# Expert layer of the third block: two dense stages against one stage that dispatches tokens to their experts

## The reference, cut to what matters

```python
t = rmsnorm(x + attention, ln2_w).reshape(-1, 256)          # 4096 tokens
probs = softmax(t @ gate_w.T)                                # 16 experts
topv, topi = top_k(probs, 6); topv = topv / sum(topv)
cw = zeros((T, 16)).at[arange(T)[:, None], topi].add(topv)
g, u = einsum('td,eid->eti', t, eg_w), einsum('td,eid->eti', t, eu_w)
routed = einsum('eti,edi,te->td', silu(g) * u, ed_w, cw)     # 176 hidden units an expert
shared = (silu(t @ sg_w.T) * (t @ su_w.T)) @ sd_w.T          # 352 hidden units
out = x + routed + shared
```

## Time and profile before

| | us |
|---|---|
| median of 3 runs (lowest, highest) | 4942.24 (4940.45, 4949.79) |
| the profiled execution's own time | 4948.9 |
| its span in the trace | 4947.2 |
| PE busy, share of the span | 4205.8, 85% |
| DVE, ACT, POOL busy | 2622.0, 2039.2, 887.2 |
| mean granted TensorE clock | 0.915 of 2.4 GHz |
| HBM traffic over the span | 23 GB/s |

### The profile page before, as it was taken

How to read it: one execution, slowest core, us unless ns; L and a number is a source line. 1 busy time by engine, 2 the same in 40 slices (tenths; PEclk the granted TensorE clock), 3 DMA queues, 4 the chain that set the end, 5 groups by cost and what they waited for, 6 DMA issues and landing times. The chain is left out here.

```text
span 4947.2 us, 74700 instructions
## 1 busy us (share of the span) xinstructions
PE 4205.8 (85%) x25323; PEld 3379.0 (68%) x25324; DVE 2622.0 (53%) x5961; ACT 2039.2 (41%) x5254; POOL 887.2 (18%) x714
## 2 busy tenths in 40 slices
PE   5886999999786874799999999699989998888692
PEld 3554899999564753678777778577767776565671
DVE  5787988987454334444443444433333333676633
ACT  4775666665122431333333333333333332666140
POOL 1002333332000420000000000122222222000145
PEclk9897999999897985899999999899999999899596
DMA  1001000000001001200000000100010000000344
GB/s 60 16 13 41 1 0 0 0 0 1 30 15 39 1 24 47 69 5 5 5 1 5 5 5 5 62 5 9 9 50 10 9 9 18 14 11 7 95 134 127
DMA packets 100239, 119.04 MB, mean 24 GB/s; under 512 B 13776, under 2 KB 81200, under 8 KB 99760
## 3 DMA queue, kind: packets, MB, share of 16 engines
q1 hardware_dynamic: 93152, 97.25, 6.1%
q0 software_dynamic: 6864, 18.75, 1.4%
HBM read 93.03 MB, written 22.94 MB: 23 GB/s over the span
## 5 line engine op out<-in xcount | busy, mean ns | idle before, releaser
L1145 ACT ACTIVATE peer_tab<-peer_sims 128x128 f32<-128x128 f32 x1024 | 305.6, 392 | 0.0
L1152 POOL TENSOR_TENSOR peer_tab<-peer_sims 128x2048 f32<-128x2048 f32 x64 | 244.6, 3842 | 290.0 <-ACT peer_sims L1129 260.8
L1200 DVE SCALAR_TENSOR_TENSOR peer_tab<-peer_tab,peer_th 128x2048 f32<-128x2048 f32 x128 | 294.9, 2346 | 0.3
L1624 DVE COPY mha_ks<-bank 128x512 f32<-128x512 f32 x128 | 88.5, 691 | 353.3 <-PE bank L1589 350.8
L1217 PE MATMUL bank<-ident,peer_tab 128*128 128x128 f32 x2048 | 247.0, 274 | 20.0 <-DVE peer_tab L1200 20.0
L1217 PEld LDWEIGHTS bank<-ident,peer_tab 128*128 128x128 f32 x2048 | 233.7, 142 | 33.6 <-DVE peer_tab L1200 21.2
L1267 PE MATMUL bank<-peer_wd,peer_hh 128*128 128x256 f32 x1024 | 242.1, 380 | 1.8 <-DVE peer_hh L1258 1.8
L1729 PE MATMUL bank<-mha_wo,mha_oT 128*128 128x256 f32 x1024 | 242.1, 379 | 0.0
L1240 PE MATMUL bank<-peer_hT,peer_wg 128*128 128x256 f32 x1024 | 241.9, 379 | 0.0
L643 DVE TENSOR_TENSOR moe2a_b<-moe2a_a,bank 128x512 f32<-128x512 f32 x104 | 71.6, 688 | 296.4 <-PE bank L556 273.2
L631 POOL TENSOR_TENSOR moe2a_hh_lo<-moe2a_hh,moe2a_hh_hi 128x512 fp32r<-128x512 f32 x104 | 141.1, 1356 | 401.4 <-ACT moe2a_hh_hi L622 385.5
(11 more groups left out here) (519 smaller groups left out, 11143.1 us busy)
## 6 DMA issues: line engine op xcount, KB each, us to landing
m_y_rows<-moe_y SPq DMA_DIRECT2D x79, 128.0 KB
att_ctxT<-in_ctxT_dram SPq DMA_DIRECT2D x32, 256.0 KB, 2.6
x<-in_x_dram SPq DMA_DIRECT2D x4, 1024.0 KB, 9.4
lin_ctxT<-in_ctxT_dram SPq DMA_DIRECT2D x16, 256.0 KB, 2.7
mem_ctxT<-in_ctxT_dram SPq DMA_DIRECT2D x16, 256.0 KB, 2.8
mem_ctx<-in_ctx_dram SPq DMA_DIRECT2D x16, 256.0 KB, 2.9
t_scratch<-mha_hTf SPq DMA_DIRECT2D x8, 512.0 KB, 2.7
moe2a_hTf<-t_scratch SPq DMA_DIRECT2D x8, 512.0 KB, 3.6
```

The lines of the kernel that those rows point to most:

```text
L1145: i = nc.scalar.activation(tab[g][h][:, b * P:(b + 1) * P], sims[:, g, h, P:2 * P], ACT.Identity, bias=sims[:, g, h, b:b + 1])
L1152: nc.gpsimd.tensor_tensor(out=tab[g][h][:].rearrange("p (a b) -> p a b", b=P), in0=sims[:, g, h, P:2 * P].unsqueeze(1).broadcast_to([P, NB ...
L1200: nc.vector.scalar_tensor_tensor(out=tab[g][h][:], in0=tab[g][h][:], scalar=th[:, g, h:h + 1], in1=tab[g][h][:], op0=ALU.is_ge, op1=ALU.mu ...
L1624: nc.vector.tensor_copy(ks[:, s % 2, :], K[:]).then_inc(ks_ready, 1)
```

## The change

- `ffn_stage` "moe2a" and "moe2b" go. One new stage, `routed_shared_stage`, takes their place.
- It makes all logits first, then six rounds of choice over all 4096 tokens, then counts, ranks and a slot for each of the 24576 pairs of token and expert. The tokens are two halves of 2048; in each, every expert's pairs are padded to blocks of 128, and the number of blocks is fixed at 111 a half (2048 x 6 / 128 + 15), 222 in all.
- POOL scatters token rows to their slots in DRAM (`places`), 192 indirect DMAs of 128 rows of 1 KB, from `src` tiles that SP loads. SP fetches each block's 128 rows by a plain DMA, stores its result in `results`, and POOL gathers the results back, 192 indirect DMAs again, 96 for each half; DVE adds each.
- Matmuls are plain fp32. An item is a block (128 rows, one expert of 176 hidden units, address from a register) or a share (128 tokens and half of the shared part, fixed addresses, 64 of them). The order is 40 shares (beside the scatter of the first half), 222 blocks, 24 shares. The adds of the first half go into DVE's loop, one in each item from item 163 on; those of the second half stand after the loop.
- In `self_attention_stage`, POOL sets a tile to zero, and SP writes it over both `places` (2 x 14.5 MB, in 14 DMAs) after its last weight load and before the first tile's store; `tail_sp` stores the normed rows in `h_rows` too (512 KB a tile), and DVE waits for these stores before it writes `xr` again.

```diff
+BLOCKS_HALF = T // 2 * 6 // P + 15
...
+        self.h_rows = nc.dram_tensor("h_rows", (T, D), FP32, kind="Internal").ap()
+        self.places = [nc.dram_tensor(f"places{h}", (BLOCKS_HALF * P, D), FP32, kind="Internal").ap() for h in range(2)]
+        self.results = [nc.dram_tensor(f"results{h}", (BLOCKS_HALF * P, D), FP32, kind="Internal").ap() for h in range(2)]
...
+        if some(t - 1):
+            dve.wait_ge(rows_stored, 16 * (t - 1))
...
+        if isinstance(t, int) and t == NT - 1:
+            dve.wait_ge(rows_stored, 16 * t)
...
     def tail_sp(sp, t):
+        sp.wait_ge(tn_ready, t + 1)
+        sp.dma_start(core.h_rows.rearrange("(g p) d -> p g d", p=P)[:, bass.ds(t * GT, GT), :], x1[:]).then_inc(rows_stored, 16)
...
+            sp.wait_ge(zero_set, 1)
+            for h in range(2):
+                places = core.places[h].rearrange("(b p) d -> p b d", p=P)
+                for b in range(0, BLOCKS_HALF, 16):
+                    n = min(16, BLOCKS_HALF - b)
+                    sp.dma_start(places[:, b:b + n, :], zero[:].unsqueeze(1).broadcast_to([P, n, D])).then_inc(places_zeroed, 16)
             tail_sp(sp, 0)
...
+            sp.wait_ge(rows_stored, 16 * NT)
+            sp.wait_ge(places_zeroed, 16 * 2 * -(-BLOCKS_HALF // 16))
...
+            nc.gpsimd.memset(zero[:], 0.0).then_inc(zero_set, 1)
...
+def routed_shared_stage(core):
...
+    E, K, I, NSH = 16, 6, 176, 2
+    I1 = I - P
+    HG = NG // 2
+    NBH = BLOCKS_HALF
+    NBLK = 2 * NBH
+    NIN, NY, NR = 6, 4, 8
+    NS1 = 40
+    NS = NG * NSH
+    ITEMS = NS + NBLK
...
+    def load_tile_sp(sp, u):
+        t = u % NT
+        if NT > u >= 2:
+            sp.wait_ge(logits_ready, u - 1)
+        if NT + 2 > u >= NT:
+            sp.wait_ge(logits_ready, u - 1)
+        if u >= NT + 2:
+            sp.wait_ge(gu_ready, share_end(t - 2))
+        sp.dma_start(hTf[u % 2][:], args["t_scratch"].rearrange("(c p) n -> p c n", p=P)[:, :, t * TILE:(t + 1) * TILE]).then_inc(hTf_in[u % 2], 16)
...
+    def load_rows_sp(sp, t):
+        if t >= 2:
+            sp.wait_ge(scattered[t - 2], 16 * GT * K)
+        sp.dma_start(src[t % 2][:], core.h_rows.rearrange("(g p) d -> p g d", p=P)[:, t * GT:(t + 1) * GT, :]).then_inc(src_in[t % 2], 16)
...
+    def scatter_pool(pool, g, k):
+        t = g // GT
+        if g % GT == 0 and k == 0:
+            pool.wait_ge(src_in[t % 2], 16 * (t // 2 + 1))
+        nc.gpsimd.indirect_dma_start(out=core.places[g // HG], out_offset=bass.IndirectOffsetOnAxis(ap=slot_u[:, k, g:g + 1], axis=0),
+                                     in_=src[t % 2][:, g % GT, :], in_offset=None).then_inc(scattered[t], 16)
+
+    def fetch_sp(sp, b):
+        if b % NBH == 0:
+            for t in range(b // NBH * NT // 2, (b // NBH + 1) * NT // 2):
+                sp.wait_ge(scattered[t], 16 * GT * K)
+        if b >= NIN:
+            sp.wait_ge(b_turned, b - NIN + 1)
+        sp.dma_start(rows[b % NIN][:], core.places[b // NBH][b % NBH * P:(b % NBH + 1) * P, :]).then_inc(rows_in[b % NIN], 16)
...
+    def block_turn_pe(pe, b):
+        pe.wait_ge(rows_in[b % NIN], 16 * (b // NIN + 1))
+        if b >= 2:
+            pe.wait_ge(hT_ready, b - 1)
+        for c in range(C):
+            i = nc.tensor.transpose(TB[b % 2][:, c * P:(c + 1) * P], rows[b % NIN][:, c * P:(c + 1) * P], core.ident[:])
+        i.then_inc(b_turned, 1)
+
+    def block_turned_act(act, b):
+        act.wait_ge(b_turned, b + 1)
+        if b >= 2:
+            act.wait_ge(gu_ready, item(b - 2) + 1)
+        for c in range(C):
+            i = nc.scalar.activation(hT[b % 2][:, c, :], TB[b % 2][:, c * P:(c + 1) * P], ACT.Copy, scale=ln2[:, c:c + 1])
+        i.then_inc(hT_ready, 1)
...
+    def gate_up_pe(pe, i, e):
+        if i >= 2:
+            pe.wait_ge(hh_ready, i - 1)
+        if static(i):
+            g, n = share(i)
+            t = g // GT
+            pe.wait_ge(hTf_in[t % 2], 16 * ((NT + t) // 2 + 1))
+            left = [hTf[t % 2][:, c, (g % GT) * P:(g % GT + 1) * P] for c in range(C)]
+            right = [wgu[:, c, E + n, :, :].rearrange("p k i -> p (k i)") for c in range(C)]
+        else:
+            b = block(i)
+            pe.wait_ge(hT_ready, b + 1)
+            left = [hT[b % 2][:, c, :] for c in range(C)]
+            right = [wgu[:, c, bass.ds(e, 1), :, :].rearrange("p e k i -> p (e k i)") for c in range(C)]
+        for c in range(C):
+            j = nc.tensor.matmul(GB[i % 2][:, 0:2 * I], left[c], right[c], start=(c == 0), stop=(c == C - 1))
...
+        nc.tensor.transpose(HB[i % 2][:, 0:P], hh[i % 2][:, 0:P], core.ident[:])
+        nc.tensor.transpose(HB[i % 2][0:I1, P:2 * P], hh[i % 2][:, P:I], core.ident[:]).then_inc(hh_turned, 1)
...
+        nc.scalar.activation(hhT[i % 2][:, 0, :], HB[i % 2][:, 0:P], ACT.Copy)
+        nc.scalar.activation(hhT[i % 2][0:I1, 1, :], HB[i % 2][0:I1, P:2 * P], ACT.Copy).then_inc(hhT_ready, 1)
...
+        nc.tensor.matmul(YB[i % 2][:, 0:D], hhT[i % 2][:, 0, :], right[0], start=True, stop=False)
+        nc.tensor.matmul(YB[i % 2][:, 0:D], hhT[i % 2][0:I1, 1, :], right[1], start=False, stop=True).then_inc(down_ready, 1)
...
+    def result_dve(dve, i):
+        dve.wait_ge(down_ready, i + 1)
+        if static(i):
+            g = share(i)[0]
+            if i:
+                dve.wait_ge(y_ready, i)
+            if i >= NS1 and g >= HG:
+                dve.wait_ge(added, HG * K)
+            nc.vector.tensor_tensor(out=group_x(g), in0=YB[i % 2][:, 0:D], in1=group_x(g), op=ALU.add).then_inc(y_ready, 1)
+        else:
+            b = block(i)
+            if b >= NY:
+                dve.wait_ge(y_out[b % NY], 16 * (b // NY))
+            nc.vector.tensor_copy(y[b % NY][:], YB[i % 2][:, 0:D]).then_inc(y_ready, 1)
+
+    def store_sp(sp, b):
+        sp.wait_ge(y_ready, item(b) + 1)
+        sp.dma_start(core.results[b // NBH][b % NBH * P:(b % NBH + 1) * P, :], y[b % NY][:]).then_inc(y_out[b % NY], 16)
+
+    def stored_pool(pool, h):
+        for i in range(NY):
+            pool.wait_ge(y_out[i], 16 * len(range(i, (h + 1) * NBH, NY)))
+
+    def return_pool(pool, n):
+        g, k = n // K, n % K
+        if n >= NR:
...
+    def add_dve(dve, n):
+        g, k = n // K, n % K
+        dve.wait_ge(back_in[n % NR], 16 * (n // NR + 1))
+        if k:
+            dve.wait_ge(added, n)
+        else:
+            dve.wait_ge(y_ready, (NS1 if (g + 1) * NSH <= NS1 else ITEMS))
+        nc.vector.scalar_tensor_tensor(out=group_x(g), in0=back[n % NR][:], scalar=w[:, k, g:g + 1], in1=group_x(g),
+                                       op0=ALU.mult, op1=ALU.add).then_inc(added, 1)
+
...
+            for u in range(NT):
+                load_tile_sp(sp, u)
+            for out, in_ in loads:
+                sp.dma_start(out, in_).then_inc(weights_in, 16)
+            for t in range(2):
+                load_rows_sp(sp, t)
+            last = 2
+            for u in range(NT, 2 * NT):
+                if static_item(u - NT) < NS1:
+                    load_tile_sp(sp, u)
+                    if u >= NT + 2 and last < NT // 2:
+                        load_rows_sp(sp, last)
+                        last += 1
+            for t in range(last, NT // 2 + 2):
+                load_rows_sp(sp, t)
+            last = NT // 2 + 2
+            for b in range(NBLK + 8):
+                if b < NBLK:
+                    fetch_sp(sp, b)
+                if b >= 8:
+                    store_sp(sp, b - 8)
+                if b in (40, 80):
+                    load_rows_sp(sp, last)
+                    last += 1
+                if b == NBLK - 1:
+                    for t in range(NT):
+                        if static_item(t) >= NS1 and share_end(t - 2) <= NS1:
+                            load_tile_sp(sp, NT + t)
+            for t in range(NT):
+                if share_end(t - 2) > NS1:
+                    load_tile_sp(sp, NT + t)
+
+        @block_.tensor
+        def _(pe):
...
+            for i in range(-1, ITEMS + 2):
+                if NS1 - 1 <= i < NS1 + NBLK - 1:
+                    block_turn_pe(pe, block(i + 1))
+                if 0 <= i < ITEMS:
+                    who_of[i] = None
+                    if not static(i):
+                        if block(i) == 0:
+                            pe.wait_ge(ids, 8)
+                        who_of[i] = pe.value_load(who_i[0:1, block(i):block(i) + 1], min_val=0, max_val=E - 1)
+                    gate_up_pe(pe, i, who_of[i])
+                if 0 <= i - 2:
+                    down_pe(pe, i - 2, who_of[i - 2])
+                if 0 <= i - 1 < ITEMS:
+                    hidden_turn_pe(pe, i - 1)
+
+        @block_.scalar
...
+            for i in range(-1, ITEMS + 2):
+                if 0 <= i - 1 < ITEMS:
+                    silu_act(act, i - 1)
+                if NS1 - 1 <= i < NS1 + NBLK - 1:
+                    block_turned_act(act, block(i + 1))
+                if 0 <= i - 2:
+                    hidden_turned_act(act, i - 2)
...
```

(22 more changed lines are left out.)

272 lines of the change are left out of this document (added).

## The result

| | median us | ratio to before, 95% interval |
|---|---|---|
| before | 4944.8 (4940.5 to 4949.8, 4 runs) | |
| the change | 5151.7 (5150.4 to 5164.3, 4 runs) | 1.0424, 1.0404 to 1.0444 |

The change makes the kernel 4.2% slower, where 1.8% faster was forecast. The profiled execution took 5150.4 us, its span 5148.6; before it was 4948.9 and 4947.2.

What follows compares the result with a forecast made beforehand. PE's stream was taken to bound the old expert stages, 1057.6 us. The new stage: 207 + 5 + 577 + 6 + 55 + 3 + 112.5 + 2.6 = 968, 89.6 less, so 4853 us; range 4823 to 4923, with 4815 to 4885 given 0.69.

Steps and rivals of the forecast that it cites:

- Forty shares of 2.3 us: Start of the new stage: shares run on PE from 90 to 182 us beside the scatter, at no cost.
- 212: Start of the new stage, until the first rows are turned: 207 us, and 5 for a held-back share and the clock.
- for 286 items I add 6: Item loop: stops of all engines, from one of 2.11 us in 79 old blocks, add 6 us.
- Four down pieces: Each block's down matmuls on PE: 0.86 us of the 2.49, the last 48 hidden units at full price.
- the chain: Block loop: row turns, ACT's copies, gate and up and the register read take 2.44 to 2.65 us; 2.60 was taken.
- a floor of 2.49: Block loop: PE's gate and up 1.18, down 0.86 and transposes 0.44 make at least 2.49 us a block.
- the second rival: Block loop: the old surplus stays, 2.85 to 3.0 us a block, 56 to 89 us more, 4909 to 4942; chance 0.12.
- Leaving costs 2.6 as before: End of the new stage: the next stage's first DMA comes 2.6 us after the adds, as before.
- the slots at 81: Start of the new stage: logits, choice, counts and ranks are done and slots known at 81 us.
- POOL's 1.25 for scatters and gathers: POOL's indirect DMAs: one starts every 1.25 us, so 96 scatters end at 202 us.
- the tail: After the loop: 88 gathers remain at DVE's end, 110 us, and 2.5 to land and add, 112.5.
- the free zero writes and row stores: Attention stage: 29 MB of zeros, 76 of 123 us on SP, and half a megabyte a tile of rows cost 0.

Runs made afterwards that it cites:

- e10: The change with a memset of 1536 elements a partition on POOL after every fourth scatter, without waiting for landing: 5003.3 us, ratio 1.0107.
- e1: The change with the last 48 hidden units of down padded by zeros to 128 rows: 5056.6 us, ratio 1.0219.
- e2: The change with ACT copying the turned hidden part before the next block's turned rows: 5108.0 us, ratio 1.0323.
- e6: The change with e1, e2, rows loaded first, 16 shares first, second half's scatters and first gathers one an item, last adds in DVE's loop: 4866.7 us, 0.9828.
- e3: The change with SP loading the rows to scatter ahead of the tiles for the shares: 5172.9 us, ratio 1.0450.

## Why the prediction was wrong

**"Forty shares of 2.3 us run from 90 to 182 meanwhile, so they are free."** This step failed, and carries most of it. It asked whether POOL's scatters slow themselves, and bounded their pitch, rightly at 1.25. It did not ask whether they slow the engines beside them. With the counts free (e10) the first block comes at 235 instead of 333, and the stops fall from 59 to 9: 148 us of the kernel's median. The rest of the 235 over 212 is the scatter, longer by the memsets: e10's shares were done at 192, and PE waited 43 us for the first rows.

**"All engines stopped once for 2.11 us, released by nothing local, in the 79 unrolled blocks; for 286 items I add 6."** The row was seen and misread. It is the first gap behind a burst, as the timeline of before shows:

```profile
4688.33 0.95 POOL L3518 DMA_INDIRECT moe_rows<-m_x_rows,moe_tok_u  x1 [0.30 <-issue]
...
4698.34 0.95 POOL L3518 DMA_INDIRECT moe_rows<-m_x_rows,moe_tok_u  x1 [0.30 <-issue]
...
4701.85 0.67 PE L3572 MATMUL bank<-moe_wd,moe_hhT 128*128 x2 [2.07 <-ACT moe_hhT L3566]
```

Nine fetches stand 1.25 us apart, and behind the last PE waits 2.07 for a copy, and POOL 2.11 for a count of PE. Before that gap the counts pass, as they do at the start of each row of scatters in the change. In the rest of that loop POOL is paced by the blocks, and no such wait comes. That the burst is its cause is read from the other runs, not tried on that stage. A rate taken per item (one stop in 79) hid the condition, a row of lists without a gap, and the change has 144 lists beside its 40 shares, in rows of 24 and 48.

**"Four down pieces (0.86; the last 48 hidden units counted at full price)."** The term was mis-sized: counted at full price it was still too cheap. Fewer rows do not merely save nothing, they cost 0.35 us an item more, 95 us of the kernel (e1), and a share is 2.61 for 2.27.

**"So the chain is 2.44 to 2.65, beside a floor of 2.49."** The chain was built from rows turned to gate and up. The late link was another: the copies of the hidden part stand behind the copies of rows, and down waits. 0.19 us a block, 44 us (e2). With both edits the pitch is the floor, so the second rival, the surplus kept, had nearly the size (3.02 against its 2.85 to 3.0) but not the cause.

**"Leaving costs 2.6 as before."** 14.3, the last 12 us.

Right were the slots at 81, POOL's 1.25 for scatters and gathers (1.27 and 1.25), the tail (114 for 112.5), the free zero writes and row stores, and the plan itself: with the faults mended, and shares and adds placed anew, the dispatch takes 4842. That this is close to the 4853 forecast is luck in part, for the parts differ: 252 us to the first block where 212 were said, and no shares behind the blocks.

## What to carry to other kernels

Work put beside indirect transfers is free only if POOL's lists have gaps: four in a row, then a memset of 1.4 us or a wait for landing, kept PE going here; six in a row cost 19 us, and twelve 67. Keep all pieces of a TensorE stream at the same number of rows, by zeros if need be. And when a wait has no local releaser, don't spread it as a rate: first look at what every other engine did in the 10 us before it.

## What was not expected of the hardware

- Beside indirect scatters 1.27 us apart, what waited for PE's counts came up to 25 us late (e6), while ACT's counts passed in under 0.1 us. The first 6 to 13 scatters of a row did no harm in the change. Gathers seem to do it as well: behind the first eight of the first half, back to back, three blocks took 16.5 us instead of 9.1.
- A matmul with 48 rows of weights behind one with 128, or the reverse, started 0.31 us after it instead of 0.22, its weight load not ahead.
- A faster scatter (e3) made the kernel slower, for its own waits had let the others go on.
